# Attention and mixture-of-experts kernel: where the products with the values of the second key block stand in TensorE's order

## What is computed

```python
x = L0_attn_x                                 # 8 x 512 x 128
xn = _layernorm(x)
# attention, 16 heads of width 8
h = xn @ W1 + b1;  q, k, v = split by head
w = einsum('bhqd,bhkd->bhqk', q, k) / 8 ** 0.5
w = softmax(causally masked w)                # 512 x 512 per head
a = einsum('bhqk,bhkd->bhqd', w, v)
attn = a @ Wp + bp
# feed-forward: a shared expert, and 2 of 8 experts chosen for each token
ffn = silu(xn @ gate.T) * (xn @ up.T) @ down.T
out = x + attn + shared + routed
```

## Time and profile before

| | us |
|---|---|
| median of 3 runs | 545.26 (543.38 to 548.12) |
| the profiled execution | 544.02 |
| its span in the trace | 541.9 |
| PE busy | 501.4 (93%) |
| DVE busy | 391.7 (72%) |
| ACT busy | 336.2 (62%) |
| POOL busy | 331.6 (61%) |

### The profile page before, as it was taken

How to read it: one execution, slowest core, us unless ns; L and a number is a source line. 1 busy time by engine, 2 the same in 40 slices (tenths; PEclk the granted TensorE clock), 3 DMA queues, 4 the chain that set the end, 5 groups by cost and what they waited for, 6 DMA issues and landing times.

```text
span 541.9 us, 13812 instructions
## 1 busy us (share of the span) xinstructions
PE 501.4 (93%) x4544; PEld 332.6 (61%) x4545; DVE 391.7 (72%) x787; ACT 336.2 (62%) x743; POOL 331.6 (61%) x392
## 2 busy tenths in 40 slices
PE   8879999999998999999989889999998899999994
PEld 3335554455454454544544389989998898877772
DVE  7796678997979978879885155556555556358886
ACT  2015788787767877777867665655555556365551
POOL 6369553442558878778788616667665574575442
PEclk9885799999979999999999999999999999999998
DMA  5434434240111544713111222222222222245555
GB/s 165 152 102 138 135 140 160 76 160 22 60 61 50 173 141 175 196 67 128 52 41 36 65 67 57 73 59 73 63 65 61 58 78 73 92 117 147 161 148 145
DMA packets 53978, 54.66 MB, mean 101 GB/s; under 512 B 6000, under 2 KB 40656, under 8 KB 53680
## 3 DMA queue, kind: packets, MB, share of 16 engines
q1 hardware_dynamic: 49248, 44.55, 26.6%
q0 software_dynamic: 4544, 9.35, 5.4%
q10 hardware_dynamic: 144, 0.20, 0.1%
HBM read 20.77 MB, written 18.68 MB: 73 GB/s over the span
## 4 chain that ended last, share of the span: by engine, by line
PE 60%; DVE 18%; issue 6%; DMA 4%; ACT 4%; another core or an unknown queue 3%; POOL 2%; ACTq 1%; DVEq 1%; SPq 0%
PE st_banks L875 12%; PE av_bank L902 11%; DVE neg_max L1583 11%; PE av_bank L1092 9%; PE mx_pair L1080 3%; PE mx_pair L1078 3%; PE mx_pair L1079 3%; DVE o_sb L1761 3%; PE mx_pair L859 2%; PE st_banks L784 2%; DMA out<-o_sb 2%; PE st_banks L790 2%; PE mx_pair L849 2%; PE st_banks L1080 1%
## 5 line engine op out<-in xcount | busy, mean ns | idle before, releaser
L1583 DVE TENSOR_REDUCE neg_max<-mx_pair 128x2 f32<-128x256 f32 (+3 forms) x256 | 200.4, 818 | 30.5 <-PE mx_pair L859 26.5
L1267 ACT ACTIVATE probs<-st_banks 128x512 f32<-128x512 f32 (+1 forms) x384 | 177.1, 528 | 59.7 <-PE st_banks L875 56.8
L875 PE MATMUL st_banks<-q_st,k_st 32*128 32x384 f32 (+3 forms) x512 | 118.3, 408 | 3.8 <-ACT probs L1267 2.5
L730 POOL DMA_INDIRECT y_tok<-y_sb,y_rows x78 | 78.1, 1001 | 68.9 <-ACT y_sb L1378 50.0
L875 PEld LDWEIGHTS st_banks<-q_st,k_st 32*128 32x128 f32 x512 | 59.5, 191 | 78.9 <-ACT probs L1267 50.1
L849 PE MATMUL mx_pair<-k_st,q_st 31*128 31x256 f32 (+3 forms) x512 | 92.0, 398 | 6.9 <-DVE neg_max L1583 5.1
L902 PE MATMUL av_bank<-probs,v_wide 128*18 128x128 f32 (+2 forms) x1272 | 97.4, 397 | 0.5 <-POOL probs L613 0.5
L654 POOL DMA_INDIRECT sorted_x<-xn_rows,slot_idx x64 | 63.6, 993 | 13.5 <-issue 12.9
L1092 PE MATMUL av_bank<-edn,hidT 128*128 (+1 forms) x468 | 59.9, 277 | 4.7 <-ACT y_sb L1378 3.5
L613 POOL TENSOR_SCALAR_AFFINE_SELECT probs<-probs 128x1024 f32<-128x1024 f32 x32 | 34.8, 1087 | 43.0 <-ACT probs L1267 42.9
L1092 PEld LDWEIGHTS av_bank<-edn,hidT 128*128 128x128 f32 (+1 forms) x468 | 55.2, 191 | 7.9 <-issue 7.9
(11 more groups left out here) (205 smaller groups left out, 900.9 us busy)
## 6 DMA issues: line engine op xcount, KB each, us to landing
sorted_x<-zeros SPq DMA_DIRECT2D x13, 387.0 KB, 3.3
xg<-sorted_x SPq DMA_DIRECT2D x39, 129.0 KB
picked<-y_tok SPq DMA_DIRECT2D x16, 256.0 KB, 3.9
q_st<-q_hi SPq DMA_DIRECT2D x14, 256.0 KB
k_st<-k_hi SPq DMA_DIRECT2D x14, 256.0 KB
egu<-in_e_gu SPq DMA_DIRECT2D x2, 1408.0 KB, 6.4
x_all<-in_x SPq DMA_DIRECT2D x8, 256.0 KB, 3.9
att_T<-a_T SPq DMA_DIRECT2D x8, 256.0 KB
```

Source lines behind the costliest of these rows:

```text
L730: pool.indirect_dma_start(y_tok, bass.IndirectOffsetOnAxis(ap=y_rows[:, t, k:k + 1], axis=0), y_sb[t % 2][:, k, :], None).then_inc(y_st[t ...
L875: ins = pe.matmul(st_banks[:, i % 3, lo:lo + w], k_st[buf][32 * j:32 * j + 32, g, kb * P:(kb + 1) * P], q_st[buf][32 * j:32 * j + 32, g, k ...
L1267: act.activation(dst, src, ACT.Exp, scale=SCALE).then_inc(st_free, 1)
L1583: ins = dve.tensor_reduce(neg_max[:, g, h:h + 2, qb], mx_pair[i % 2][:, :, lo:lo + (qb + 1) * P], AX.X, ALU.max, negate=True)
```

## The change

In the PE program the call `values(s - 1, 1)` moves from behind the third unit to behind the fifth, ahead of `values(s - 1, 2)`.

```diff
                 if s < 0:
                     keep_awake(spare, AWAKE)
-                if valued:
-                    values(s - 1, 1)
                 if scored:
                     scores(s, (4,))
...
                 if maxima:
                     max_masks(s + 2, 4)
                 if valued:
+                    values(s - 1, 1)
                     values(s - 1, 2)
                 if scored:
                     scores(s, (8,))
```

## The result

| | before | after |
|---|---|---|
| median | 546.69 us (543.38 to 549.73, 4 runs) | 574.57 us (571.37 to 578.90, 4 runs) |
| ratio, after to before | | 1.0574, 95% interval 1.0521 to 1.0627 |
| profiled execution, its span | 544.02, 541.9 | 573.18, 571.0 |
| mean granted clock of that span | 0.965 | 0.938 |
| attention part, from its first maxima to its last product with values | 292.9 | 323.6 |

A forecast was written before the change was run, and what follows sets the result against it. No engine was saturated; they wait for each other through two small rings. Step delays of 15.9 us less 1.1 for late wakes gave 14.8 on 544.0, so 558.8, stated as 559.0; range 549 to 567.

The forecast's parts named there:

- What a run costs: Behind the fifth unit, the new run of 640 columns takes 0.77 + 0.55 - 0.12 = 1.20 us.
- The place behind the third unit is free: With a projection, ACT's two exponentials cover key block 1's run of 0.77 us there, so moving it gains 0.
- Delay of a step with a projection: The sixth unit starts 0.65 us later, with no gain against it; 17 such steps make 11.0.
- Gain in a step without a projection: The fifth unit's slot 11 can start about 0.27 us earlier, leaving a delay of 0.38; 9 steps make 3.4.
- The delay reaches the end: At the end of each step, the next step moves by the whole delay, through ACT's av_bank copy in even steps.
- The late wakes: In steps 17, 21 and 25 ACT takes slot 6 late; removing the run may return 0.7 us each, half counted: 1.1.
- The sum: Over 31 steps in the loop: 11.0, 3.4, 0.9 and 0.6 make 15.9 us, less 1.1 gives 14.8.
- Slower still, by the clock: Rival: PE's new waits in the fourth unit bring four more 1.2 GHz stretches of 2.6 us each, making 569; chance 0.08.
- Much of it absorbed: Rival: PE's later arrival falls into existing waits behind the turn and late wakes, leaving +3.3 us, 547.3; chance 0.12.
- Only the switches count: Rival: PE itself is the bound, so each step shrinks by one units-values switch, 0.12 us, to 540.3; chance 0.04.
- Faster: Rival: fourth unit and projection start 0.77 us earlier, winning DVE's 17.3 us idle time and PE's 3.7: 523; chance 0.05.

The follow-up runs named there:

- e1: The kernel before with the products of key block 1 left out inside the loop (31 runs of values): 561.39 us, 3.4% slower.
- e6: The kernel before with key block 1's products behind the third unit replaced in place by three products of zero: ratio 0.9945.
- e5: The changed kernel with three products of zero where key block 1 was, waiting for the zero tile only ahead of the loop: ratio 1.0215.
- e8: The kernel before with more start-up products (keep_awake) around the first steps: gave nothing, for the 5 to 8 us expected.
- e7: The changed kernel with one product of zero where key block 1 was: within 0.3 us of e5's time.
- e10: The changed kernel with one product of zero behind the third unit, on the same chip as e9: 563.50 us.
- e9: The changed kernel measured again, on the same chip as e10: 573.65 us.
- e11: The kernel before with key block 1 moved only in the 11 steps without work behind the fourth unit: 1.9% slower.
- e12: The kernel before with key block 1 moved only in the 20 steps with work behind the fourth unit: 3.4% slower.

## Why the prediction was wrong in size, step by step

**What a run costs: right.** 1.21 and 1.20 us for 640 columns, for 1.20.

**The place behind the third unit is free: right, but for the clock.** The projection comes 1.71 behind the third unit (forecast 1.75), e1's steps at full clock 3 to 7 are as long as before's, and e6 is no slower. Delay of a step with a projection: 0.62 on the chip of e5 to e8, for 0.65; 0.60 as a mean in the two first traces, which is partly luck, as their single steps scatter from 0.03 to 1.55.

**Gain in a step without a projection: right, in its own terms.** 0.33 to 0.37 in e7, for 0.38. In the two first traces the five steps at full clock grew 0.12, 0.49, 0.49, 0.62 and 1.11, on average more than forecast. In step 20 the run of values starts 2.53 behind the third unit (232.22 - 229.69), the forecast 2.82 - 0.27 = 2.55; so the mechanism is there.

**The delay reaches the end: right, with an exception I did not name.** In steps 6, 7, 8 and 11 DVE has routing work, and they grew 0.49, 0.46, 0.12 and 0.03 between the two first traces: 1.2 us less than I had counted. That the routing work is the reason is not shown: steps 5 and 12 have some too, and grew 0.61 and 0.33 in e7. Steps 2 and 3, which I had at 0.3, grew 0.6 each.

**The late wakes: moved, not removed.** I took back 1.1 us for steps 17, 21 and 25. Steps 17 and 25 grew 0.49 and 0.29, so they did give back 0.13 and 0.33 of the 0.62 that e7 shows for them. Step 21 was at the lower clock for 3.4 us and can't be read. But step 18 grew 1.55 and step 26 1.11. In step 18 of the changed kernel, PE's mask products of the sixth unit and DVE's maxima of it:

```profile
216.59 0.33 PE L859 MATMUL mx_pair<-mask_k,mask_q 32*128 32x256 f32 x2
```

```profile
217.90 0.69 DVE L1582 TENSOR_REDUCE neg_max<-mx_pair 128x2 f32<-128x512 f32 x1 [1.65 <-PE mx_pair L859]
```

The products end at 216.92, and DVE takes them at 217.90, nearly 1 us later. In steps 2 to 28 of e5 to e8 no maximum of DVE and no exponential of ACT that waited for PE began 0.45 us or more behind the end of PE's last product for it.

**The sum without the clock: right on one chip, 3 to 4 us short on the other. The step that failed is "The sum": it has no term for TensorE's clock, which stands only under the rival "Slower still, by the clock".** On the chip of e5 to e8 the delay is 14.0 us in steps 2 to 28 and 14.5 to 15.3 in all, for 14.8. In the first pair of traces 34.2 us more at 1.2 GHz, at 0.34 to 0.39 each, make 11.6 to 13.3 of the 30.7 us, and leave 17.4 to 19.1 to the delay. The clock is the larger part of the miss. I had the price: 0.37 per us at the lower level from the earlier trace rows, against 0.34 to 0.39 here over the whole part. Two things I had not. I set the clock beside the forecast as another outcome, at 0.08, when it was a second term of the same sum. And the 10 us that I gave it as such a rival I then left out of the range, which ended at 567. With 14.8 and 12 I would have said 571; the runs had 574.57. (A slip beside it: 558.8 on the profiled execution's scale is 560.0 on the median's, and I said 559.0.)

**Why I gave it 0.08.** "The new waits are shorter than a unit" was my argument against, and it was no argument. The earlier trace rows had PE busy 97%; by my own reckoning the changed kernel does 0.12 us less PE work in a step that is 0.65 longer, which brings some 9% of new idle time into steps of 8 us. And the profile of before held the warning: a spell at 1.2 GHz at 152.1, behind a stretch with PE busy 6.34 of 7 us, 91%. I had both numbers and did not set them side by side. As it turned out, the changed kernel has 31.06 of 35, 89%, in its steady stretch.

The Trainium skill (TensorE: Matmul & The Clock Gate, HAM oscillation) tells of a matmul kernel whose waits for data, of 3 to 5 us, put it back to half rate in every tile. The repeated spells here are like it, the waits are not: between 64 and 310 us of the changed kernel PE never stands idle for 1 us at a time (0.97 at most), and yet five spells begin there. The same page (Terms) prices the loss at the time at the lower level x (1 - K/N), 0.5 us per us; here, where ACT, DVE and POOL set part of the pace and keep theirs at either level, e10 against e9 shows 0.34 as a whole and 0.28 to 0.50 in single steps.

**The other rivals fell.** "Much of it absorbed": the transposes behind the turn gave nothing back; on the chip of e5 to e8 the odd steps 9, 15, 17, 19, 21, 23 and 25 grew 0.61 to 0.65, as the even step 10 did. "Only the switches count": no step at full clock got shorter. "Faster": DVE's idle time ahead of the 768s did go, 4.3 to 0.5, as that rival said, and the larger loss ahead of the sixth unit stood against it; the turning point it named, a projection under 1.7 behind the third unit, was not passed.

**Left open.** What decides when the clock falls: six spells of e9, from 98.6 us on, all begin 1.4 us later than in the first trace of the changed kernel, whose first maxima begin 1.3 earlier, so the program has a large part in it. But e7 and e10 are one program on two chips, with 27.3 and 51.2 us at 1.2 GHz, so it is not the program alone. And e1 fell after a stretch with PE busy 95%, while the changed kernel stayed up through others with less, so the busy share alone does not tell. Of the 3 to 4 us of delay that the first chip has over that of e5 to e8, over 2 lie in steps -1 and 1: the 3.5 us by which these grew, less 1.2 for 3.4 us more at 1.2 GHz. They seem to go with the early spell and not with the moved run: step 1 took 15.7 to 15.8 us in the three traces in which that spell began at 39 to 41 us (the changed kernel, e9, e10), and 12.4 to 13.1 in the five in which it began at 36 and lasted 24 us (before, e1, e7, e11, e12), of which e7 and e12 have the run moved in step 1 and the others not. For the rest, the late wakes can be named in some steps, not added up. And why they show on some chips and not on another stays open.

No variant here beats the kernel before by over 1%; e6, which does by 0.5%, leaves products out.

## What to carry to other kernels

Work that stands where its engine would wait anyway is free; moved next to other work it costs its whole length, less what the neighbours have buffered, so before two runs are joined to save a switch (0.12 us here), look at what each was hiding behind. Then price TensorE's clock as a term of the sum, not as an unlikely alternative: where a change opens idle time on a TensorE that is nearly full, and the profile before has spells at the lower level already, the range reaches over several more of them. Where the clock does fall, idle time that can't be closed with useful products is worth one run with a product of zeros in it: here it gave back 1.8% of the changed kernel. It was not tried on the kernel before as it stands.

## What the runs showed of the hardware

- Taking TensorE work out can slow a kernel: 31 runs of products fewer cost 3.4% (e1), and products of zeros in their place put it back (e6, 0.9945).
- A us at 1.2 GHz cost 0.34 us in this interleaved kernel as a whole, and 0.28 to 0.50 in single steps (e9 over e10).
- Idle times under 1 us, with PE busy 89%, went with repeated falls to 1.2 GHz; one filler of 0.32 us a step took the time there from 71.7 to 51.2 us (e9, e10).
- Merging two runs of values saved 0.12 us of PE's time, and a single 512-column product of zeros between two units took 139.67 - 139.35 = 0.32 us, three of them 0.75: 0.21 each, and the same 0.11 once. The Trainium skill (TensorEngine Tiling (Array Packing), Key Properties) has a drain on a change of the tiling mode and gives no figure; that this fixed part is that drain fits, and no run here separates it.
- The same kernel took 525.2 us on one chip and 543.7 to 546.7 in the three other sets of runs, at nearly the same granted clock. On that chip the part behind the attention took 215 us for 231, and the late wakes are absent (step 17: 8.32 us in e8, 9.01 in the first trace of before, with the same work).
